# Second layer's routing of a two-layer transformer kernel: the first eight token tiles' deviations, normalisation, transposes and router products placed in the tail of the second attention

## The chip, the cores and the metric

The kernel runs on one core of one Trainium2 chip. The metric is the device time of one execution in microseconds. Three runs of the kernel before gave a median of 1085.19 us (1085.11 to 1086.78). One more execution was recorded by the profiler: it took 1081.04 us, of which 1079.3 us lie between its first and its last instruction (the span). All rows below are of that execution, and their times count from the span's start.

Engines: PE is TensorE (matmuls and transposes; PEld its weight loads), DVE VectorE, ACT ScalarE, POOL GpSimd, SP SyncE (it issues the plain transfers).

## The reference, cut to what matters

2048 tokens of 256 channels (8 sequences of 256) pass through two layers, each an attention over a small context and a mixture of experts with a shared expert:

```python
x = x + tanh(g_xattn[0]) * xattn0(layernorm(x), ctx)       # linear attention
x = x + tanh(g_ffn[0])   * ffn0(layernorm(x))              # 8 experts, top 2
x = x + tanh(g_xattn[1]) * xattn1(layernorm(x), ctx)       # 16 heads, quantised softmax attention
x = x + tanh(g_ffn[1])   * ffn1(layernorm(x))              # 16 experts, top 4

def layernorm(x): return (x - mean(x)) / sqrt(var(x) + 1e-5)

def ffn1(x):
    logits = x @ router_w.T                     # 16 logits a token
    vals, idx = top_k(softmax(logits), 4)       # weights of the chosen experts
    shared = silu(x @ sgate.T) * (x @ sup.T) @ sdown.T
    return sum over the 4 chosen experts(w * expert(x)) + sigmoid(x @ se_gate.T) * shared
```

The change concerns the seam between `xattn1` and `ffn1`: the last `layernorm`, and `logits`.

## The kernel before

**Tiles.** The tokens are 16 tiles of 128 (`NT` = 16); `x_sb` holds them all, 128 partitions by 16 tiles by 256 channels. Each engine has its own program, written out by hand in Python; the order of the calls is the order on the engine, and the engines meet only at semaphores. No scheduler moves anything.

**The second attention** (`attn1_pe`, `attn1_act`, `attn1_dve`, `attn1_pool`) is a software pipeline of 136 steps `s`. A step stands for two heads of one tile (`PAIRS` = 8, so eight steps a tile, 128 steps `NQ` of heads, eight of run-out). In a step PE computes the logits of two heads (L1178) and transposes the probabilities of an earlier step (L1188) and multiplies them with the values (L1200), DVE finds the maxima (L1303) and copies transposed probabilities (L1308), ACT takes the exponentials (L1262), and POOL rounds them to integers (L1606), twice a step. Beside this, once in 16 steps, a pair of tiles `G` gets its queries ready (POOL L1554 to L1579, PE L1082 to L1099), and a pair of tiles `o` is finished: `normalised` divides by the sums (L1313, L1315), PE transposes (L1210), ACT and DVE split into high and low halves (`output_high` L1273, `output_low` L1322), PE projects (`project`, L256 and L263), DVE adds the result to x (`update`, L1328) and takes its mean and variance (`stats`, L240 and L243). `output_step(s, j, tail)` says in which step a pair has its turn; the last pair, `o` = 7, is taken in the run-out at `s = NQ + tail`. POOL also splits the second layer's weights into halves, a third of an item in each step in which it has no queries to do (L1407 to L1412), until they run out.

**The seam.** After the last `update` and `stats`, DVE adds the epsilon (`stats_end`, L247), POOL raises to the power -1/2 (`inverse_deviation`, L1679), and `route_dve`, `route_act`, `route_pe` do the routing. First DVE makes `nmr`, minus mean by deviation, for all 16 tiles (L419). Then, for each of eight pairs of tiles `j`: ACT normalises the even tile (L403) and DVE the odd one (L422) into `xnf`; PE transposes both (four fp32 transposes, L359) into PSUM bank `j % 2`; ACT copies the high halves into `xnT` (L407), DVE subtracts for the low halves (L430); PE multiplies with the router's weights (`mm3`, 12 matmuls of 17 columns, L256), and DVE copies the logits to `lg` (L434). SP stores each pair of normalised tiles to the token table in HBM. Before the routing PE, ACT and DVE meet at a barrier: `meet(…, 3)` is a drain and a wait for the other two.

**After it** the shared expert's gate and up products (`shared_gate_up`, L256 on `sgu`) start once all eight pairs' logits are copied (`r_lgc`), beside DVE's choice of experts (`choose_dve` and what follows, L446 to L566), after which the gathers for the experts start on POOL (L631).

Of the kernel before, what the change touches and what calls it, by code (L numbers as in the profile page):

```python
# [10 lines left out]
ALU = mybir.AluOpType  # L11
# [4 lines left out]
C = D // P  # L16
HEADS, HD = 16, 16
MAGIC = 1.5 * 2.0 ** 23
SW = 256.0
# [13 lines left out]
def gated_flamingo(nc, a, out):  # L33
# [30 lines left out]
    with ExitStack() as ctx:  # L64
# [184 lines left out]
        EARLY = LATE = 4  # L249
        STATS_STEPS = (4, 8, 14)  # L250
# [99 lines left out]
        def route_pe(pe, l):  # L350
            n = E[l] + 1
            for j in range(NT // 2 + 1):
                if j < NT // 2:
                    at_least(pe, r_xn[l], 0, j + 1)
                    at_least(pe, r_xd[l], 0, j + 1)
                    at_least(pe, r_xl[l], 0, j - 1)
                    for c in range(C):
                        for i in range(2):
                            last = nc.tensor.transpose(PS[:, j % 2, c * TB + i * P:c * TB + (i + 1) * P],  # L359
                                                       xnf[:, 2 * j + i, c * P:(c + 1) * P], idf[:, :])  # L360
                    last.then_inc(r_xT[l].sem, 1)
                if j >= 1:
# [34 lines left out]
        def route_act(act, l):  # L397
            act.wait_ge(rstd_ready, 2 + 3 * l)
            at_least(act, r_nm[l], 0, 1)
            for j in range(NT // 2 + 1):  # L400
                if j < NT // 2:
# [3 lines left out]
                if j >= 1:  # L405
# [10 lines left out]
        def route_dve(dve, l):  # L416
            n = E[l]
            dve.wait_ge(rstd_ready, 2 + 3 * l)
            nc.vector.scalar_tensor_tensor(nmr[:, :], mv[:, :, 0], -1.0, rstd[:, :], ALU.mult, ALU.mult)\  # L419
                .then_inc(r_nm[l].sem, 1)  # L420
            def normalise(t):
                nc.vector.tensor_scalar(xnf[:, t, :], x_sb[:, t, :], mv[:, t, 0:1], rstd[:, t:t + 1],  # L422
                                        ALU.subtract, ALU.mult).then_inc(r_xd[l].sem, 1)
            normalise(1)
            for j in range(NT // 2 + 1):
                if j + 1 < NT // 2:
                    normalise(2 * j + 3)
                if j < NT // 2:
                    at_least(dve, r_xh[l], 0, j + 1)
                    nc.vector.tensor_tensor(xnT[:, 1, :, j * TB:(j + 1) * TB], PS[:, j % 2, :].rearrange("p (c n) -> p c n", c=C),  # L430
                                            xnT[:, 0, :, j * TB:(j + 1) * TB], ALU.subtract).then_inc(r_xl[l].sem, 1)
                if j >= 1:
                    at_least(dve, r_lg[l], 0, j)
                    nc.vector.tensor_scalar(lg[:, 2 * j - 2:2 * j, 0:n + 1],  # L434
                                            PS[:, 2 + (j - 1) % 2, 0:2 * (n + 1)].rearrange("p (i e) -> p i e", i=2),
                                            1 / SW, None, ALU.mult).then_inc(r_lgc[l].sem, 1)
# [733 lines left out]
        def attn1_pe(pe):  # L1170
# [82 lines left out]
            meet(pe, 3)  # L1253

        def attn1_act(act):
# [39 lines left out]
            meet(act, 3)  # L1295

        def attn1_dve(dve, combine):
# [32 lines left out]
            for s in range(STEPS):  # L1330
# [27 lines left out]
                o = output_step(s, 18, 7)  # L1358
                if o is not None:
                    stats(2 * o, 2 * o + 1)  # L1360
            stats_end(0, NT)
            meet(dve, 3)
# [239 lines left out]
        def attn1_pool(pl, inverse_deviation):  # L1602
# [7 lines left out]
            for s in range(NQ):  # L1610
                integers(s)
                if s == 3:
                    inverse_deviation(3, EARLY, NT)
                if all(query_step(s, j) is None for j in (0, 8, 9, 10, 11)) and parts < 3 * len(items):
                    split_part(pl, parts // 3, parts % 3)
                    parts += 1
# [14 lines left out]
        def _(pl):  # L1631
# [56 lines left out]
            inverse_deviation(4)  # L1688
# [6 lines left out]
        def _(act):  # L1695
# [90 lines left out]
            route_act(act, 1)  # L1786
# [3 lines left out]
        def _(dve):  # L1790
# [124 lines left out]
            route_dve(dve, 1)  # L1915
# [3 lines left out]
        def _(pe):  # L1919
# [105 lines left out]
            route_pe(pe, 1)  # L2025
# [49 lines left out]
```

## Time and profile before

| what | value |
|---|---|
| median of 3 runs | 1085.19 us |
| profiled execution | 1081.04 us |
| its span | 1079.3 us |
| PE busy | 855.4 us, 79% of the span |
| DVE busy | 751.1 us, 70% |
| POOL busy | 644.7 us, 60% |
| ACT busy | 460.2 us, 43% |
| chain that ended last, by engine | PE 40%, POOL 18%, DVE 13%, issue 10% |
| of it at L359 (routing transposes) | PE 1% |
| of it at L1606 (POOL's integers, `sb_wk` and `sb_wkh`) | 3% |

Busy time is an average over stages that differ: the share of an engine in the span tells nothing of who holds up the seam. The second attention lies from about 370 us to 716 us, the routing from 722 us to 736 us, the choice of experts to 785 us. The chain of work that ended last is the view that tells, at each moment, whose work the end waited for; the timeline of an engine gives for each group of instructions its start, its length, and in brackets how long the engine idled before and what released it.

### The profile page before, as it was taken

What the parts mean: (1) busy time and instruction counts of PE and PEld (TensorE: products, weight loads), DVE (VectorE), ACT (ScalarE), POOL (GpSimd) and SP (SyncE); (2) the same over time, 40 slices, a digit from 0 to 9 for tenths busy, and PEclk for the clock granted to TensorE, in tenths of its full rate; (3) what the DMA queues carried; (4) which work ended last, traced back from release to release, by engine and by line L of the source; (5) the groups of instructions that cost most, each with busy time, mean ns of one, the idle gap of its engine ahead of it and who ended that gap; (6) DMA issues with size and microseconds to landing.
All of it is one profiled execution on the core that took longest, in us unless ns stands there. A gap on an engine that the chain in (4) does not pass through costs nothing.

```text
span 1079.3 us, 21036 instructions
## 1 busy us (share of the span) xinstructions
PE 855.4 (79%) x6928; PEld 572.4 (53%) x6929; DVE 751.1 (70%) x1527; ACT 460.2 (43%) x993; POOL 644.7 (60%) x851
## 2 busy tenths in 40 slices
PE   4489668699989877787777787859769999997764
PEld 2267545477655444445445455535557777763432
DVE  5779667467567777797787787947956767754445
ACT  3455244233222357666657666825123333321201
POOL 4586781667275878888888887610054444415563
PEclk9689759799999856687786786857679999997988
DMA  7021142244321100000110000011024444423341
GB/s 249 25 77 34 56 125 63 76 142 150 112 87 50 47 15 14 15 21 22 28 41 25 16 4 1 2 39 40 6 83 136 126 136 124 139 81 97 98 117 59
DMA packets 55445, 75.04 MB, mean 70 GB/s; under 512 B 11069, under 2 KB 46657, under 8 KB 55361
## 3 DMA queue, kind: packets, MB, share of 16 engines
q1 hardware_dynamic: 44992, 44.82, 13.0%
q0 software_dynamic: 10368, 29.14, 10.0%
q8 instruction: 48, 0.79, 0.3%
q14 instruction: 37, 0.30, 0.1%
HBM read 51.45 MB, written 22.49 MB: 69 GB/s over the span
## 4 chain that ended last, share of the span: by engine, by line
PE 40%; POOL 18%; DVE 13%; issue 10%; ACT 5%; POOLq 5%; DVEq 4%; DMA 2%; another core or an unknown queue 1%; SPq 0%; ACTq 0%
PE PS L256 24%; PE PS L679 3%; POOL sb_xnf L656 3%; POOL sb_xnf L631 3%; DVE sb_slotv L1303 3%; POOL sb_wk L1606 2%; PE PS L703 2%; PE PS L732 2%; PE PS L1188 2%; PE PS L1178 2%; ACT sb_wk L1262 2%; POOL sb_wkh L1606 1%; POOL sb_region L1412 1%; PE PS L359 1%; DMA sb_x_sb<-x 1%
## 5 line engine op out<-in xcount | busy, mean ns | idle before, releaser
L631 POOL DMA_INDIRECT sb_xnf<-token_table,sb_ids x120 | 115.8, 965 | 180.1 <-DVE sb_ids L565 87.9
L256 PE MATMUL PS<-sb_region,sb_wkh 88*128 (+1 forms) x1440 | 210.7, 297 | 5.4 <-issue 2.8
L1303 DVE TENSOR_REDUCE sb_slotv<-PS 128x1 f32<-128x512 f32 x256 | 164.0, 683 | 42.6 <-PE PS L1178 42.6
L256 PEld LDWEIGHTS PS<-sb_region,sb_wkh 88*128 88x128 f16 (+1 forms) x1440 | 136.9, 99 | 57.9 <-issue 12.8
L656 POOL DMA_INDIRECT sb_xnf<-slot_table,sb_place x96 | 96.5, 1005 | 90.6 <-DMA slot_table<-sb_wa 39.0
L256 PE MATMUL PS<-sb_xnT,sb_sgu 128*128 128x512 f16 x528 | 132.0, 402 | 2.1 <-issue 1.1
L679 PE MATMUL PS<-sb_sdn,sb_wkh 128*128 128x256 f16 (+1 forms) x576 | 79.5, 293 | 46.5 <-DVE sb_wkh L846 32.6
L1262 ACT ACTIVATE sb_wk<-PS,sb_slotv 128x512 f32<-128x512 f32 x128 | 86.9, 686 | 36.8 <-DVE sb_slotv L1303 33.6
L761 ACT ACTIVATE sb_wk<-PS 128x512 f32<-128x512 f32 (+1 forms) x48 | 28.6, 595 | 166.9 <-PE PS L256 139.4
L679 PEld LDWEIGHTS PS<-sb_sdn,sb_wkh 128*128 128x128 f16 (+1 forms) x576 | 57.1, 103 | 70.9 <-DVE sb_wkh L846 41.6
L1606 POOL TENSOR_SCALAR sb_wk<-sb_wk 128x512 f32<-128x512 f32 x128 | 79.5, 621 | 20.5 <-ACT sb_wk L1262 11.7
L256 PEld LDWEIGHTS PS<-sb_xnT,sb_sgu 128*128 128x128 f16 x528 | 53.3, 103 | 68.2 <-issue 19.6
L1308 DVE TENSOR_SCALAR sb_wkh<-PS 128x1024 f16<-128x1024 f16 x112 | 76.9, 687 | 10.5 <-PE PS L1200 9.8
L780 ACT ACTIVATE sb_wkh<-PS 128x512 f16<-128x512 f32 x60 | 35.8, 596 | 106.9 <-PE PS L703 97.1
L875 DVE SCALAR_TENSOR_TENSOR sb_wk<-PS,sb_sm,sb_wk 128x176 f32<-128x176 f32 x120 | 42.6, 397 | 51.7 <-ACT sb_wk L789 45.6
L839 DVE SCALAR_TENSOR_TENSOR sb_wk<-PS,sb_wk 128x512 f32<-128x512 f32 (+1 forms) x48 | 33.2, 692 | 64.5 <-ACT sb_wk L761 52.9
L1188 PE MATMUL PS<-sb_idh,sb_wk 128*128 128x128 f16 x512 | 58.8, 270 | 12.2 <-POOL sb_wk L1606 6.7
L789 ACT ACTIVATE sb_wk<-PS 128x352 f32<-128x352 f32 x60 | 27.8, 463 | 88.8 <-PE PS L256 75.4
L859 DVE TENSOR_TENSOR sb_wkh<-PS,sb_wkh 128x512 f16<-128x512 f32 x60 | 41.4, 690 | 33.1 <-ACT sb_wkh L780 32.0
L1188 PEld LDWEIGHTS PS<-sb_idh,sb_wk 128*128 128x128 f16 x512 | 39.6, 119 | 40.6 <-issue 32.8
L1262 ACT ACTIVATE sb_wkh<-PS,sb_slotv 128x512 f32<-128x512 f32 x64 | 43.4, 683 | 29.9 <-DVE sb_slotv L1303 29.2
L1412 POOL TENSOR_TENSOR sb_region<-sb_stg,sb_region 128x704 f16<-128x704 f32 (+1 forms) x32 | 43.0, 1344 | 20.9 <-issue 19.9
(281 smaller groups left out, 1816.1 us busy)
## 6 DMA issues: line engine op xcount, KB each, us to landing
slot_table<-sb_wa SPq DMA_DIRECT2D x60, 256.0 KB
sb_stg<-gu SPq DMA_DIRECT2D x24, 352.0 KB, 3.0
sb_stg<-dn SPq DMA_DIRECT2D x24, 176.0 KB
token_table<-sb_xnf SPq DMA_DIRECT2D x16, 256.0 KB, 3.6
sb_stg<-sgu SPq DMA_DIRECT2D x8, 352.0 KB, 6.6
sb_x_sb<-x SPq DMA_DIRECT2D x1, 2048.0 KB, 12.1
out<-sb_x_sb SPq DMA_DIRECT2D x16, 128.0 KB
sb_xnf<-token_table,sb_ids POOLq DMA_INDIRECT x120
```

Of the source, the lines that this page charges most:

```text
L256: last = nc.tensor.matmul(out_, lhs(i, c), rhs(j, c), start=(c == 0 and n == 0 and not begun), stop=(c == C - 1 and n == 2 and not more))
L631: nc.gpsimd.indirect_dma_start(xg[l][:, 2 * (g % XR) + n, :], None, xw[l][:, :], bass.IndirectOffsetOnAxis(ap=ids[:, 2 * g + n:2 * g + n + ...
L656: nc.gpsimd.indirect_dma_start(yr[l][r][:, k, :], None, ys[l][:, :], bass.IndirectOffsetOnAxis(ap=place[:, k, t:t + 1], axis=0))\
L679: last = nc.tensor.matmul(PS[:, 4 + i // 2, i % 2 * D:(i % 2 + 1) * D], wkh[0:r, HR * h + v, i * P:(i + 1) * P], sdn[0:r, j, k, :], start= ...
L859: nc.vector.tensor_tensor(wkh[:, 2 * (s % 2) + 1, :], PS[:, 4 + s % 2, :], wkh[:, 2 * (s % 2), :], ALU.subtract).then_inc(e_xl[l].sem, 1)
L875: last = nc.vector.scalar_tensor_tensor(wk1[:, 2 + u, n * EI:(n + 1) * EI], PS[:, 2 * u + n, EI:EG], wv[u][:, n:n + 1], wk1[:, u, n * EI:( ...
L1188: last = nc.tensor.transpose(bank[:, (h * KT + k) * P:(h * KT + k + 1) * P], h_p[s % NE][:, h, k * P:(k + 1) * P], idh[:, :])
L1262: nc.scalar.activation(h_e[s % NE][:, h, :], PS[:, 2 * u + h, :], ACT.Exp, bias=h_nb[u][:, h:h + 1], accum_out=o_sum[v][:, head:head + 1]) ...
L1303: nc.vector.tensor_reduce(h_nb[u][:, h:h + 1], PS[:, 2 * u + h, :], AX, ALU.max, negate=True).then_inc(h_max, 1)
L1308: nc.vector.tensor_scalar(h_T[s % 2], PS[:, 4 + s % 2, :].bitcast(F16), -RB, None, ALU.add).then_inc(h_pc_dve, 1)
L1412: nc.gpsimd.tensor_tensor(lo, w, hi, ALU.subtract).then_inc(stg_split[n % 4], 1)
L1606: nc.gpsimd.tensor_scalar(h_e[s % NE][:, h], h_e[s % NE][:, h], 255.0, MAGIC + RB_BITS, ALU.mult, ALU.add).then_inc(h_int, 1)
```

## The change

The routing is cut into two halves of four pairs. `route_pe`, `route_act` and `route_dve` take a first and an end pair. The first half (tiles 0 to 7) stands at the end of the attention functions, in the place of the barrier `meet(…, 3)`; the second half (tiles 8 to 15) stands where the whole stood. For the first half:

- DVE closes the variances of tiles 0 to 7 (`stats_end(0, 8)`) in step 83, after `stats` of pair 3;
- POOL raises them to the power -1/2 in step 90, between the integers and the query work of that step; the second call, for tiles 8 to 15, is where the call for all tiles was;
- in step 133 (`NQ + 5`), between `output_low(7)` and `update(7)`, DVE makes `nmr` of tiles 0 to 7 and normalises the four odd tiles; the low halves and logits of the four pairs come after the last `stats_end`;
- ACT's and PE's first half follow `output_high(7)` and `project(7)`.

`stats` of a pair `o` below 7 moves from step 18 + 16(o+1) to the next step, so that it stands behind `normalised` rather than before it.

```diff
@@ -247,6 +247,7 @@
...
+        ROUTE_EARLY = 8
@@ -347,10 +348,10 @@
...
-        def route_pe(pe, l):
+        def route_pe(pe, l, first=0, end=NT // 2):
...
-            for j in range(NT // 2 + 1):
-                if j < NT // 2:
+            for j in range(first, end + 1):
+                if j < end:
@@ -359,7 +360,7 @@
...
-                if j >= 1:
+                if j > first:
@@ -394,15 +395,15 @@
...
-        def route_act(act, l):
-            act.wait_ge(rstd_ready, 2 + 3 * l)
-            at_least(act, r_nm[l], 0, 1)
-            for j in range(NT // 2 + 1):
-                if j < NT // 2:
+        def route_act(act, l, first=0, end=NT // 2):
+            act.wait_ge(rstd_ready, 2 + 3 * l + (first > 0))
+            at_least(act, r_nm[l], 0, 1 + (first > 0))
+            for j in range(first, end + 1):
+                if j < end:
...
-                if j >= 1:
+                if j > first:
@@ -413,27 +414,34 @@
...
-        def route_dve(dve, l):
+        def deviations_route(dve, l, first, end):
+            dve.wait_ge(rstd_ready, 2 + 3 * l + (first > 0))
+            nc.vector.scalar_tensor_tensor(nmr[:, first:end], mv[:, first:end, 0], -1.0, rstd[:, first:end], ALU.mult, ALU.mult)\
+                .then_inc(r_nm[l].sem, 1)
+
+        def normalise_dve(l, t):
+            nc.vector.tensor_scalar(xnf[:, t, :], x_sb[:, t, :], mv[:, t, 0:1], rstd[:, t:t + 1],
+                                    ALU.subtract, ALU.mult).then_inc(r_xd[l].sem, 1)
+
+        def low_logits_dve(dve, l, j, first, end):
...
+            if j < end:
+                at_least(dve, r_xh[l], 0, j + 1)
+                nc.vector.tensor_tensor(xnT[:, 1, :, j * TB:(j + 1) * TB], PS[:, j % 2, :].rearrange("p (c n) -> p c n", c=C),
+                                        xnT[:, 0, :, j * TB:(j + 1) * TB], ALU.subtract).then_inc(r_xl[l].sem, 1)
+            if j > first:
+                at_least(dve, r_lg[l], 0, j)
+                nc.vector.tensor_scalar(lg[:, 2 * j - 2:2 * j, 0:n + 1],
+                                        PS[:, 2 + (j - 1) % 2, 0:2 * (n + 1)].rearrange("p (i e) -> p i e", i=2),
+                                        1 / SW, None, ALU.mult).then_inc(r_lgc[l].sem, 1)
+
+        def route_dve(dve, l, first=0, end=NT // 2):
+            deviations_route(dve, l, 2 * first, 2 * end)
+            normalise_dve(l, 2 * first + 1)
+            for j in range(first, end + 1):
+                if j + 1 < end:
+                    normalise_dve(l, 2 * j + 3)
+                low_logits_dve(dve, l, j, first, end)
@@ -1250,7 +1258,7 @@
...
-            meet(pe, 3)
+            route_pe(pe, 1, 0, ROUTE_EARLY // 2)
@@ -1292,7 +1300,7 @@
...
-            meet(act, 3)
+            route_act(act, 1, 0, ROUTE_EARLY // 2)
@@ -1355,11 +1363,18 @@
...
-                o = output_step(s, 18, 7)
+                o = output_step(s, 19 + 0, 7)
...
-            stats_end(0, NT)
-            meet(dve, 3)
+                if o == ROUTE_EARLY // 2 - 1:
+                    stats_end(0, ROUTE_EARLY)
+                if s == NQ + 5:
+                    deviations_route(dve, 1, 0, ROUTE_EARLY)
+                    for t in range(1, ROUTE_EARLY, 2):
+                        normalise_dve(1, t)
+            stats_end(ROUTE_EARLY, NT)
+            for j in range(ROUTE_EARLY // 2 + 1):
+                low_logits_dve(dve, 1, j, 0, ROUTE_EARLY // 2)
@@ -1611,6 +1626,8 @@
...
+                if s == (ROUTE_EARLY // 2 + 1) * GSTEPS + 10:
+                    inverse_deviation(4, 0, ROUTE_EARLY)
@@ -1685,7 +1702,7 @@
...
-            inverse_deviation(4)
+            inverse_deviation(5, ROUTE_EARLY, NT)
@@ -1783,7 +1800,7 @@
...
-            route_act(act, 1)
+            route_act(act, 1, ROUTE_EARLY // 2)
@@ -1912,7 +1929,7 @@
...
-            route_dve(dve, 1)
+            route_dve(dve, 1, ROUTE_EARLY // 2)
@@ -2022,7 +2039,7 @@
...
-            route_pe(pe, 1)
+            route_pe(pe, 1, ROUTE_EARLY // 2)
```

On DVE, from `update` of pair 6 to the first odd tiles (names: `sb_slotv` are the sums' reciprocals, `sb_xnT` in L1315 and L1323 the attention's output, `sb_ve` variance plus epsilon). Before:

```order
L1328 SCALAR_TENSOR_TENSOR sb_x_sb<-PS,sb_tgw,sb_x_sb 128x512 [waits o_y]
L240 BN_STATS sb_bst<-sb_x_sb 128x6 x2
L243 BN_AGGR sb_mv<-sb_bst 128x2 x2
L1313 RECIPROCAL sb_slotv<-sb_slotv 128x16 [waits o_T,h_pv]
L1315 TENSOR_TENSOR sb_xnT<-PS,sb_slotv 128x256
L1322 SCALAR_TENSOR_TENSOR sb_xnT<-PS,sb_xnT 128x512 [waits o_y,o_hi]
L1328 SCALAR_TENSOR_TENSOR sb_x_sb<-PS,sb_tgw,sb_x_sb 128x512 [waits o_y]
L240 BN_STATS sb_bst<-sb_x_sb 128x6 x2
L243 BN_AGGR sb_mv<-sb_bst 128x2 x2
L247 TENSOR_SCALAR sb_ve<-sb_mv 128x16
L419 SCALAR_TENSOR_TENSOR sb_nmr<-sb_mv,sb_rstd 128x16 [waits rstd_ready,phase]
```

and with the change:

```order
L1336 SCALAR_TENSOR_TENSOR sb_x_sb<-PS,sb_tgw,sb_x_sb 128x512 [waits o_y]
L1321 RECIPROCAL sb_slotv<-sb_slotv 128x16 [waits o_T,h_pv]
L1323 TENSOR_TENSOR sb_xnT<-PS,sb_slotv 128x256
L240 BN_STATS sb_bst<-sb_x_sb 128x6 x2
L243 BN_AGGR sb_mv<-sb_bst 128x2 x2
L1330 SCALAR_TENSOR_TENSOR sb_xnT<-PS,sb_xnT 128x512 [waits o_y,o_hi]
L419 SCALAR_TENSOR_TENSOR sb_nmr<-sb_mv,sb_rstd 128x8 [waits rstd_ready]
L423 TENSOR_SCALAR sb_xnf<-sb_x_sb,sb_mv,sb_rstd 128x256 x4
L1336 SCALAR_TENSOR_TENSOR sb_x_sb<-PS,sb_tgw,sb_x_sb 128x512 [waits o_y]
L240 BN_STATS sb_bst<-sb_x_sb 128x6 x2
L243 BN_AGGR sb_mv<-sb_bst 128x2 x2
L247 TENSOR_SCALAR sb_ve<-sb_mv 128x8
```

The two rows of `normalised` (L1313, L1315; now L1321, L1323) stand ahead of the statistics of pair 6, and `nmr` with four odd tiles stands ahead of the last `update`; the barrier (`phase`) is gone.

On DVE, the routing of the pairs after that. Before, each pair's odd tile is normalised between the low halves:

```order
L422 TENSOR_SCALAR sb_xnf<-sb_x_sb,sb_mv,sb_rstd 128x256 x2
L430 TENSOR_TENSOR sb_xnT<-PS,sb_xnT 128x2x256 [waits r_xh]
L422 TENSOR_SCALAR sb_xnf<-sb_x_sb,sb_mv,sb_rstd 128x256
L430 TENSOR_TENSOR sb_xnT<-PS,sb_xnT 128x2x256 [waits r_xh]
L434 TENSOR_SCALAR sb_lg<-PS 128x34 [waits r_lg]
L422 TENSOR_SCALAR sb_xnf<-sb_x_sb,sb_mv,sb_rstd 128x256
```

With the change the low halves and logits of four pairs follow one another, and then the second half begins with its own `nmr`, which can't start before the last logits of the first half are copied:

```order
L430 TENSOR_TENSOR sb_xnT<-PS,sb_xnT 128x2x256 [waits r_xh] x2
L434 TENSOR_SCALAR sb_lg<-PS 128x34 [waits r_lg]
L430 TENSOR_TENSOR sb_xnT<-PS,sb_xnT 128x2x256 [waits r_xh]
L434 TENSOR_SCALAR sb_lg<-PS 128x34 [waits r_lg]
L430 TENSOR_TENSOR sb_xnT<-PS,sb_xnT 128x2x256 [waits r_xh]
L434 TENSOR_SCALAR sb_lg<-PS 128x34 [waits r_lg] x2
L419 SCALAR_TENSOR_TENSOR sb_nmr<-sb_mv,sb_rstd 128x8 [waits rstd_ready]
L423 TENSOR_SCALAR sb_xnf<-sb_x_sb,sb_mv,sb_rstd 128x256 x2
```

On POOL, step 90 of the attention (L1606, now L1621, are the integers; L1564 to L1568, now L1579 to L1583, the rounding of queries). Before:

```order
L1606 TENSOR_SCALAR sb_xnf<-sb_xnf 128x512 [waits h_exp] x2
L1564 TENSOR_SCALAR sb_xnT<-sb_xnT 128x256 [waits q_frac]
L1566 TENSOR_SCALAR sb_xnT<-sb_xnT 128x256
L1568 TENSOR_TENSOR sb_xnT<-sb_xnT,sb_slotv 128x256
L1606 TENSOR_SCALAR sb_wkh<-sb_wkh 128x512 [waits h_exp] x2
L1577 TENSOR_SCALAR sb_xnT<-sb_xnT 128x16x16 [waits q_T]
```

and with the change, one instruction more:

```order
L1621 TENSOR_SCALAR sb_xnf<-sb_xnf 128x512 [waits h_exp] x2
L1696 TENSOR_TENSOR sb_rstd<-sb_ve,sb_mhalf 128x8 [waits stats_ready]
L1579 TENSOR_SCALAR sb_xnT<-sb_xnT 128x256 [waits q_frac]
L1581 TENSOR_SCALAR sb_xnT<-sb_xnT 128x256
L1583 TENSOR_TENSOR sb_xnT<-sb_xnT,sb_slotv 128x256
L1621 TENSOR_SCALAR sb_wkh<-sb_wkh 128x512 [waits h_exp] x2
L1592 TENSOR_SCALAR sb_xnT<-sb_xnT 128x16x16 [waits q_T]
```

## Rows read from the trace of the kernel before

**Rows 1.** Stretches: us; busy and count by engine; granted clock, DMA share, GB/s.

```profile
420.00:670.00 250.00, 193.85 (x2032) 124.60 (x2031) 201.54 (x358) 165.94 (x416) 213.55 (x341) 0.75 0.07 20
670.00:702.00 32.00, 26.75 (x327) 17.27 (x325) 31.69 (x58) 25.66 (x69) 20.34 (x33) 0.89 0.01 2
```

**Rows 2.** Timeline of POOL, steps 90, 91: start, length, idle before, releaser.

```profile
617.71 1.31 POOL L1606 TENSOR_SCALAR sb_xnf<-sb_xnf 128x512 f32<-128x512 f32 x2
...
620.89 1.31 POOL L1606 TENSOR_SCALAR sb_wkh<-sb_wkh 128x512 f32<-128x512 f32 x2
```

**Rows 3.** Chain of waits, end of step 91: start, length, instruction.

```profile
623.30 0.68 POOL sb_xnT L1579
624.02 1.04 PE PS L1099 x8
```

**Rows 4.** Timeline of DVE, end of the attention and the routing.

```profile
707.13 0.75 DVE L1328 SCALAR_TENSOR_TENSOR sb_x_sb<-PS,sb_tgw,sb_x_sb 128x512 f32<-128x512 f32 x1 [1.06 <-PE PS L263]
707.98 0.75 DVE L240 BATCH_NORM_STATS2 sb_bst<-sb_x_sb 128x6 f32<-128x256 f32 x2
...
708.97 0.22 DVE L1313 RECIPROCAL sb_slotv<-sb_slotv 128x16 f32<-128x16 f32 x1
709.26 0.42 DVE L1315 TENSOR_TENSOR sb_xnT<-PS,sb_slotv 128x256 f32<-128x256 f32 x1
...
716.23 0.75 DVE L1328 SCALAR_TENSOR_TENSOR sb_x_sb<-PS,sb_tgw,sb_x_sb 128x512 f32<-128x512 f32 x1 [4.02 <-PE PS L263]
...
718.58 0.17 DVE L247 TENSOR_SCALAR sb_ve<-sb_mv 128x16 f32<-128x16 f32 x1 [0.43 <-issue]
721.86 0.18 DVE L419 SCALAR_TENSOR_TENSOR sb_nmr<-sb_mv,sb_rstd 128x16 f32<-128x16 f32 x1 [3.10 <-POOL sb_rstd L1679]
...
724.60 0.69 DVE L430 TENSOR_TENSOR sb_xnT<-PS,sb_xnT 128x512 f16<-128x512 f32 x1 [1.92 <-ACT sb_xnT L407]
...
735.92 0.19 DVE L434 TENSOR_SCALAR sb_lg<-PS 128x34 f32<-128x34 f32 x1 [0.48 <-PE PS L256]
```

**Rows 5.** Timeline of PE, the last projections and the routing.

```profile
712.27 1.46 PE L256 MATMUL PS<-sb_wqp,sb_xnT 128*128 128x256 f16 x6 [1.41 <-DVE sb_xnT L1322]
...
722.85 1.94 PE L359 MATMUL PS<-sb_idf,sb_xnf 128*128 128x128 f32 x8 [6.65 <-ACT sb_xnf L403]
...
725.71 1.09 PE L359 MATMUL PS<-sb_idf,sb_xnf 128*128 128x128 f32 x4
...
731.65 1.09 PE L359 MATMUL PS<-sb_idf,sb_xnf 128*128 128x128 f32 x4
```

**Rows 6.** POOL's power by shape: count, busy, mean ns, idle before.

```profile
L1679 POOL TENSOR_TENSOR sb_rstd<-sb_ve,sb_mhalf 128x4 f32<-128x4 f32 x1 | 1.1, 1127 | 0.0
...
L1679 POOL TENSOR_TENSOR sb_rstd<-sb_ve,sb_mhalf 128x12 f32<-128x12 f32 x1 | 2.3, 2306 | 0.1
```

**Rows 7.** Timeline of PE, logits of step 115.

```profile
678.26 0.39 PE L1178 MATMUL PS<-sb_wkv,sb_xnT 64*128 64x512 f16 x1 [0.28 <-ACT sb_xnf L1262]
```

**Rows 8.** Chain of waits, first gate and up product of layer 1.

```profile
736.17 5.31 PE PS L256 x12
```

**Rows 9.** Stretches in which the granted clock rose, layer 1 and layer 0.

```profile
740.00:742.00 2.00, 2.00 (x6) 0.73 (x5) 0.00 (x0) 0.49 (x1) 0.00 (x0) 0.52 0.00 0
...
158.00:162.00 4.00, 4.00 (x11) 1.43 (x10) 3.33 (x6) 0.00 (x0) 3.64 (x5) 0.54 1.11 340
```

**Rows 10.** Timeline of PE, first gate and up product of layer 0.

```profile
157.36 3.17 PE L256 MATMUL PS<-sb_xnT,sb_sgu 128*128 128x512 f16 x7 [0.27 <-DVE sb_lg L434]
```

**Rows 11.** Timeline of PE, a later gate and up product of layer 1.

```profile
753.01 2.75 PE L256 MATMUL PS<-sb_xnT,sb_sgu 128*128 128x512 f16 x12
```

More of the change, by code:

```diff
@@ L414, in softmax_act @@
             nc.scalar.activation(sm[:, 1, :], lg[:, :, E[l]], ACT.Exp, scale=-1.0).then_inc(r_exp[l].sem, 1)
-        def route_dve(dve, l):
-            n = E[l]
[L418 to L436, printed above, removed]
```

## The prediction

> **What bounds the kernel now.** I read the chain of waits first, then the timeline of each engine at the two places where instructions are put in.
>
> At the seam the chain hops between engines. The last projections of the attention begin at 712.27 [rows 5], `update(7)` waits 4.02 us for them and starts at 716.23, `stats_end` ends at 718.75, POOL's power keeps DVE idle for 3.10 us, and `nmr` starts at 721.86 [rows 4]. PE has then idled 6.65 us and starts its first routing transposes at 722.85 [rows 5]. The last logits are copied at 735.92 + 0.19 = 736.11 [rows 4], and the first gate and up product starts at 736.17 [rows 8]. The eight pairs run in two PSUM banks: pair 2's transposes start at 725.71 and pair 6's at 731.65 [rows 5], so four pairs take 5.94 us, 1.485 us each. That is latency from engine to engine, not one engine's work.
>
> In the attention itself POOL sets the pace until its weight splits run out: from 420 to 670 us it is busy 213.55 of 250 us, more than DVE's 201.54 or PE's 193.85; from 670 to 702 us it has only 20.34 us of work in 32, and DVE is busy for 31.69 [rows 1]. Step 90, where the change puts the power of eight columns, starts at 617.71, step 91 at 620.89, and neither shows idle time before it [rows 2]. The chain of waits passes through POOL's last query instruction of step 91 at 623.30 and PE's transposes at 624.02 that waited for it [rows 3].
>
> **The seam, term by term.** The barrier costs nothing now: it is over while POOL computes the power. Nor is its removal worth anything, except that work may stand before it.
>
> First, `normalised` goes ahead of the statistics of pair 6. Those hold DVE from 707.98 to 708.97, where the reciprocal starts; the divided tile starts at 709.26 and everything up to `update(7)` hangs on it [rows 4]. Without them the reciprocal starts at 707.98, so the tail moves up by 0.99 us: projections from 711.3, `update(7)` at 715.24 instead of 716.23, `stats_end` over at 717.76. The moved statistics lie beside PE's transposes and ACT's copy. `nmr` and the four odd tiles (some 0.4 us each, before `update(7)`) lie beside the projections, which take 3.9 us; ACT's first two tiles too.
>
> Second, the first half. PE's transposes of pairs 0 and 1 follow the projections directly: 715.2 to 717.2, by the 1.94 us that these eight take now [rows 5]. DVE comes to the low half of pair 0 after `stats_end`, at about 717.8. From there to the last logits it now takes 736.11 - 724.60 = 11.51 us for eight pairs [rows 4]; four pairs less are 5.94 us less, so 5.57 us, until 723.35. POOL's power for tiles 8 to 15 is done by 719.6 and hidden.
>
> Third, the second half starts afresh, since its `nmr` is queued on DVE behind the last logits of the first. From `nmr` to the transposes takes 722.85 - 721.86 = 0.99 us as now, and from the transposes to the last logits 13.26 - 5.94 = 7.32 us [rows 4, 5]. It ends at 723.35 + 0.99 + 7.32 = 731.7, against 736.11: 4.4 us gained. Had the halves been joined without restart, it would be some 2 us more; this restart is what the cut gives back.
>
> **The attention, term by term.** The power of eight columns doesn't occur in the trace. Its nearest rows are four columns at 1127 ns and twelve at 2306 ns [rows 6]; halfway is 1.72 us, and with a gap of 0.07 us between POOL instructions 1.8 us. On an engine without idle time at that place, and with the chain through its next query instructions, it delays everything behind it in full, since PE's transposes at 624.02 wait for it and DVE and ACT wait for PE. I charge 1.8 us. The bounds are 0 (hidden in a POOL idle later on) and 2.4 us (the twelve-column row and a gap). It also splits the later power, whose saving is not counted, being hidden.
>
> The statistics of pairs 0 to 5 move by a step too. In steps 35 to 99 POOL is the pace, and I charge nothing: DVE's total is the same, and they fill a step in which DVE has no probabilities to copy. In step 115 DVE is the pace [rows 1]: it comes to the maxima 0.99 us earlier and finds the second head's logits ready only at 678.26 + 0.39 = 678.65 [rows 7]. I charge 0.2 us; bounds -0.3 (smoother) to +0.5.
>
> **The clock.** PE's first gate and up product is on the chain, 5.31 us for 12 matmuls [rows 8]; a later one takes 2.75 [rows 11]. The granted clock averages 0.52 of full speed over 740 to 742 [rows 9], so it rose from 1.2 to 2.4 GHz at about 741.9, 5.7 us after the product began. In layer 0 the same product began at 157.36 [rows 10] and the average over 158 to 162 is 0.54, a rise at 161.7, 4.3 us after [rows 9]. Were it 1.4 us earlier here, work done in that time would go twice as fast, 0.7 us saved. I take 0.3 us of gain, bounds -0.7 to +0.7.
>
> **The sum.** -4.4 + 1.8 + 0.2 - 0.3 = -2.7 us. Against the profiled execution's own 1081.04 us that is 1078.3. The median of the three timed runs is 1085.19, 4.15 us above it, so I forecast 1082.5 us. What a measurement of this kernel can tell from no change is about 0.2%, 2.2 us: faster is below 1083.0, slower above 1087.4. The forecast lies half a microsecond from that edge.
>
> **Rivals.**
>
> *The clock comes early.* Projections and the transposes of pairs 0 and 1 now make 3.9 + 1.94 = 5.9 us of unbroken PE work, as long as the stretch of gate and up after which the clock rose. PE's 6.65 us of idleness between them is gone. At 2.4 GHz the transposes (0.97 us a pair) and router products (about 0.5 us) of a pair of pairs would be 0.7 us shorter on the chain; six remaining pairs give 2.1, and the first gate and up product 5.31 - 2.75 = 2.6. Then the time is 1082.5 - 4.7 = 1077.8. Against it: the routing of today, PE busy at most times from 722.85 on, did not raise it. The Trainium skill, "TensorE: Matmul & The Clock Gate", Part 1, says that the throttled clock is the default and sustained activity releases it. By that rule the unbroken stretch speaks for this rival; the trace agrees in so far as the rise came within gate and up.
>
> *The power is hidden.* If POOL's idle time after step 103 took up the delay, 1.8 us come back: 1080.7. For it: POOL has 11.66 us of idleness from 670 to 702 [rows 1]. Against it: PE waited for POOL's query work before that, and DVE, the pace from 670 on, waits for PE.
>
> *The gain is eaten without a loss.* The power costs 2.4, step 115 0.5, the clock rises late (+0.7): -4.4 + 3.6 = -0.8, 1084.4.
>
> *Slower: the statistics delay the next maxima.* In each of six steps 16k + 3 DVE now has the division and 0.99 us of statistics before the maxima of the next step, on which ACT's exponentials and POOL's integers hang. If none of it is covered by what was gained a step earlier, 6 x 0.99 = 5.9 us, and the time is 1082.5 - 0.2 + 5.9 = 1088.2. It decides from 0.45 us a step (the gain of 2.7 is gone then). For it: DVE is busy 81% of the time even where POOL is the pace. Against it: the statistics stood before a maximum already, one step earlier, and the step behind has no more work than it had.
>
> **How the numbers follow.** Forecast 0.60, with its own range 1080.9 to 1084.2; clock early 0.12; power hidden 0.08; gain eaten 0.12; slower 0.08. Of the forecast's 0.60 I put 0.36 below 1083.0; with 0.11 of the early clock and 0.07 of the hidden power, faster is 0.54. Slower is 0.06, the rest, 0.40, is within 0.2%. The range 1079.0 to 1086.5 leaves out the far ends of the early clock and of the slower case.
>
> **What would show it.** Right: a power of about 1.7 us on POOL in step 90, and steps from 91 on later by as much, to the last maxima; then PE's first fp32 routing transposes directly behind the last projections; a pause of PE of about 1.3 us before the first router product and of about 1.5 us between the halves; first gate and up product 4.4 us earlier relative to the attention's last maxima. Wrong: POOL idle behind step 90 that shrinks by the power's length, maxima of steps 36, 52 and so on that start later than their logits, a clock of 2.4 GHz within the routing, or a second half that starts without waiting for the first.

## The result, and the profile after

The changed kernel took 1075.70 us (median of 20 runs, 1071.44 to 1084.90), the kernel before 1081.68 us beside it (20 runs, 1075.83 to 1086.78). The ratio is 0.9959, 95% interval 0.9940 to 0.9978, or -4.4 us (-6.5 to -2.4). A second measurement, described below, gave 0.9997 (0.9963 to 1.0031). Weighted by their intervals the two make 0.9968 (0.9951 to 0.9985), -3.4 us. The profiled execution took 1071.44 us (span 1069.7), by chance the shortest of its runs; 5.5 of the 9.6 us by which it is ahead of the profiled execution before lie ahead of the second attention (POOL's first integers at 367.70, before at 373.16), where nothing was changed.

DVE's timeline of the changed kernel, from `update` of pair 6 to the end of the routing (start, length, group, idle before and releaser):

```profile
706.87 0.75 DVE L1336 SCALAR_TENSOR_TENSOR sb_x_sb<-PS,sb_tgw,sb_x_sb 128x512 f32<-128x512 f32 x1 [0.23 <-PE PS L264]
707.54 0.24 DVE L1321 RECIPROCAL sb_slotv<-sb_slotv 128x16 f32<-128x16 f32 x1
...
714.37 0.75 DVE L1336 SCALAR_TENSOR_TENSOR sb_x_sb<-PS,sb_tgw,sb_x_sb 128x512 f32<-128x512 f32 x1 [2.65 <-PE PS L264]
...
716.44 1.28 DVE L430 TENSOR_TENSOR sb_xnT<-PS,sb_xnT 128x512 f16<-128x512 f32 x2
...
720.86 0.19 DVE L434 TENSOR_SCALAR sb_lg<-PS 128x34 f32<-128x34 f32 x1 [0.48 <-PE PS L257]
720.97 0.16 DVE L419 SCALAR_TENSOR_TENSOR sb_nmr<-sb_mv,sb_rstd 128x8 f32<-128x8 f32 x1
...
729.06 0.19 DVE L434 TENSOR_SCALAR sb_lg<-PS 128x34 f32<-128x34 f32 x1 [0.49 <-PE PS L257]
```

The reciprocal now starts 0.67 us after `update(6)`; before it was 708.97 - 707.13 = 1.84 [rows 4]. From `update(7)` to the last logits it is 14.88 us against 19.88. The 3.10 us of idleness before `nmr` [rows 4] are gone: the second half's `nmr` has no idle time in front of it, but it stands, as forecast, behind the first half's last logits.

PE's timeline there:

```profile
708.33 0.66 PE L1218 MATMUL PS<-sb_idf,sb_xnT 128*128 128x128 f32 x4 [1.01 <-DVE sb_xnT L1323]
...
713.73 0.60 PE L264 MATMUL PS<-sb_brow,sb_ones_h 1*128 1x256 f16 x2
714.26 1.90 PE L360 MATMUL PS<-sb_idf,sb_xnf 128*128 128x128 f32 x8
717.18 0.46 PE L257 MATMUL PS<-sb_rw,sb_xnT 128*128 128x17 f16 x12 [1.03 <-DVE sb_xnT L430]
717.50 0.64 PE L360 MATMUL PS<-sb_idf,sb_xnf 128*128 128x128 f32 x4
...
721.88 1.97 PE L360 MATMUL PS<-sb_idf,sb_xnf 128*128 128x128 f32 x8 [1.05 <-ACT sb_xnf L404]
...
724.77 1.09 PE L360 MATMUL PS<-sb_idf,sb_xnf 128*128 128x128 f32 x4
```

The first transposes follow the projections without a gap, where PE idled for 6.65 us [rows 5]. Four transposes take 0.64 us at 717.50 and 1.09 at 724.77: for a while TensorE ran at 2.4 GHz. So it did in the first row, the attention's own transposes of pair 7, which take 0.66 us here and 1.12 in the kernel before. The granted clock (the last figure but two), in stretches of 1 us:

```profile
716.00:717.00 1.00, 0.16 (x2) 0.00 (x0) 0.89 (x4) 1.00 (x4) 0.38 (x1) 1.00 0.00 0
...
719.00:720.00 1.00, 0.45 (x12) 0.40 (x12) 1.00 (x3) 0.55 (x1) 0.00 (x0) 0.69 0.19 55
```

It is at full speed from 716.0, behind PE's unbroken stretch that began at 710.41, until some 719.4. On POOL, step 90 now holds the power:

```profile
616.04 1.32 POOL L1621 TENSOR_SCALAR sb_xnf<-sb_xnf 128x512 f32<-128x512 f32 x2
617.44 1.65 POOL L1696 TENSOR_TENSOR sb_rstd<-sb_ve,sb_mhalf 128x8 f32<-128x8 f32 x1
...
620.98 1.32 POOL L1621 TENSOR_SCALAR sb_wkh<-sb_wkh 128x512 f32<-128x512 f32 x2
```

The step takes 4.94 us against 3.18 [rows 2]. The routing's last copy releases the first gate and up product, on the chain of waits:

```profile
729.06 0.20 DVE sb_lg L434
...
729.31 4.59 PE PS L257 x12
```

It takes 4.59 us, 0.72 less than before [rows 8]. That is no gain of the change: in the three other profiles of the kernel before (below) the same product takes 4.2 to 5.0 us, in those of the changed kernels 4.0 to 5.3, as the granted clock rises sooner or later within it.

### The profile page after: what moved, and what is told of

Its sections match the earlier page's. It is cut to its first block, busy times and chain, and to the rows that moved or that the text cites. A ratio compares the mean times of both kernels' runs of the same rounds, so it can differ in the third digit from the quotient of the medians.

```text
span 1069.7 us, 21037 instructions
## 1 busy us (share of the span) xinstructions
PE 849.5 (79%) x6928; PEld 572.6 (54%) x6929; DVE 755.6 (71%) x1529; ACT 462.2 (43%) x993; POOL 645.5 (60%) x852
## 4 chain that ended last, share of the span: by engine, by line
PE 35%; POOL 18%; DVE 15%; issue 11%; ACT 5%; POOLq 5%; DVEq 4%; another core or an unknown queue 4%; DMA 3%; SPq 0%; ACTq 0%
PE PS L257 21%; POOL sb_xnf L639 3%; DVE sb_slotv L1311 3%; POOL sb_xnf L664 2%; POOL sb_wk L1621 2%; PE PS L687 2%; PE PS L740 2%; PE PS L711 2%; POOL sb_region L1427 2%; PE PS L1196 2%; PE PS L1186 2%; ACT sb_wk L1270 1%; POOL sb_wkh L1621 1%; DMA sb_x_sb<-x 1%
## 5 line engine op out<-in xcount | busy, mean ns | idle before, releaser
L257 PE MATMUL PS<-sb_xnT,sb_sgu 128*128 128x512 f16 x528 | 127.8, 395 | 1.1 <-DVE sb_lg L434 0.6
L1621 POOL TENSOR_SCALAR sb_wk<-sb_wk 128x512 f32<-128x512 f32 x128 | 79.8, 623 | 24.1 <-ACT sb_wk L1270 15.4
```

The source lines that it names most:

```text
L257: last = nc.tensor.matmul(out_, lhs(i, c), rhs(j, c), start=(c == 0 and n == 0 and not begun), stop=(c == C - 1 and n == 2 and not more))
L1621: nc.gpsimd.tensor_scalar(h_e[s % NE][:, h], h_e[s % NE][:, h], 255.0, MAGIC + RB_BITS, ALU.mult, ALU.add).then_inc(h_int, 1)
```

## The experiments

After the first measurement (row "changed") came three groups of runs, each on its own chip beside runs of the kernel before: 1079.46 us in the first (changed again, power late, statistics only, gap), 1081.66 in the second (before again, four early tiles, halves joined, statistics back), 1057.26 in the third (the last two rows and two single executions of the kernel before). Ratios compare within a group. Each kernel also left one profile. *Tail* is from `update(6)` to the reciprocal, *routing* from `update(7)` to the first gate and up product, *attention* from POOL's first integers to those of step 127.

| kernel | ratio to before (95%) | tail | routing | step 90 | attention |
|---|---|---|---|---|---|
| before, page shown ahead | | 1.84 | 19.94 | 3.18 | 329.1 |
| before again, second group | 1.0001 (0.9970-1.0033) | 1.83 | 19.95 | 3.19 | 332.6 |
| before, two executions, third group | | 1.84, 1.83 | 19.94 | 3.20, 3.19 | 335.1, 333.6 |
| changed | 0.9959 (0.9940-0.9978) | 0.67 | 14.94 | 4.94 | 335.3 |
| changed again | 0.9997 (0.9963-1.0031) | 0.67 | 15.89 | 4.93 | 337.8 |
| power late | 0.9949 (0.9914-0.9984) | 0.67 | 14.92 | 3.19 | 336.4 |
| statistics only | 1.0015 (0.9979-1.0050) | 0.67 | 19.95 | 3.21 | 334.4 |
| gap on PE | 0.9988 (0.9951-1.0026) | 0.67 | 16.41 | 4.92 | 337.6 |
| four early tiles | 0.9977 (0.9938-1.0016) | 0.67 | 15.95 | 3.19 | 337.1 |
| statistics back, power late | 0.9958 (0.9927-0.9990) | 1.83 | 15.90 | 3.20 | 334.8 |
| halves joined, power late | 0.9960 (0.9923-0.9997) | 0.67 | 13.15 | 3.19 | 336.9 |
| joined, again | 0.9942 (0.9914-0.9971) | 0.67 | 13.14 | 3.19 | 337.1 |
| joined, only pair 6's statistics | 0.9925 (0.9895-0.9956) | 0.67 | 13.63 | 3.20 | 332.2 |

The medians have intervals of 3 to 4 us each way; the columns from the profiles, tail, routing and step 90, repeat within 0.05 us as long as the clock is the same. So the steps of the argument are judged by the profiles.

**The changed kernel again.**

> The changed kernel once more, for a second profile. Theory A (the gain is latency taken off the seam, and a single execution differs by when the clock is granted): step 90 on POOL again takes 1.7 to 1.8 us more than step 106; from the start of POOL's last integers to the first gate and up product 26.5 to 29.5 us against 33.9 before; and the time before the second attention differs from the first profile by some us with nothing changed there. Theory B (the change also shortens something outside the seam, as the 5.4 us that this profile was ahead at the attention's start would suggest): the start of the attention is again some 5 us earlier than before's. Time 3 to 6 us under before.

1079.26 us, a ratio of 0.9997. Its routing shows no rise of the clock, and so is 0.95 us longer than in the first profile:

```profile
714.00:721.00 7.00, 4.58 (x21) 2.19 (x22) 3.94 (x13) 1.69 (x3) 0.00 (x0) 0.65 0.22 76
721.00:737.00 16.00, 11.29 (x130) 9.21 (x130) 9.68 (x28) 8.88 (x15) 1.65 (x1) 0.50 0.29 99
```

The granted clock stays at 0.50 throughout the routing. The early clock is thus not a property of the changed program: of eight profiles with the unbroken stretch on PE it came in four. In these four the clock had last fallen 5.2 to 5.4 us before `update(7)`; in the other four 4.5 to 4.9 or 6.2 to 6.4 us before it. The expectation's theory B falls: the attention starts at 370.31 us here, in the four profiles of the kernel before at 365.5 to 373.2.

**Power late.** Power of tiles 0 to 7 behind POOL's last integers:

```diff
-                if s == (ROUTE_EARLY // 2 + 1) * GSTEPS + 10:
-                    inverse_deviation(4, 0, ROUTE_EARLY)
...
+            inverse_deviation(4, 0, ROUTE_EARLY)
             inverse_deviation(5, ROUTE_EARLY, NT)
```

> POOL's power of tiles 0 to 7 stands behind the last integers, where POOL is idle, rather than in step 90. If the power in step 90 delays all behind it (the prediction's term of 1.8 us): step 90 takes 3.2 us as before and the kernel is 1.8 us faster than the changed one, some 0.55 to 0.6% under before. If POOL's idle time later on hides it: the same time as the changed kernel.

1074.45 us. Step 90 falls back to 3.19 us and the seam stays as it was (14.92), so in the attention the power cost 1.75 us and in the tail it costs nothing: POOL idles there. The kernel is 4.8 us under the changed kernel of its group, where 1.8 were expected; the intervals of the two overlap, so the times neither show the 1.8 us nor contradict them.

**Statistics only.** The kernel before with one number changed:

```diff
-                o = output_step(s, 18, 7)
+                o = output_step(s, 19, 7)
```

> The kernel before with one edit: the statistics of pairs 0 to 6 one step later. If the prediction's term holds: the division of tile 15 starts 0.3 us after the update of pair 6 ends rather than 1.4, the seam is 1.0 us shorter, steps 115 and 116 together are within 0.3 us of before, total 0.7 to 1.0 us faster (0.1%). If the statistics delay the next maxima (the slower rival): steps 35, 51, 67, 83, 99 show up to 0.99 us more each on POOL and the kernel is 2 to 5 us slower. If the order also spares steps outside the tail, it is over 1.5 us faster.

1080.94 us: no difference that this can tell. The maxima that the slower rival named are not late: POOL's steps 35, 51, 67, 83 and 99, and the step behind each, are as long as in the kernel before, within 0.02 us in all fourteen profiles. Step 54 is longer, 3.24 us, where it takes 2.89 to 2.92 at the same clock with the statistics in their old place (more on it below). The tail is 1.17 us shorter and the routing as before, so the remaining 4.0 to 5.0 us of the seam belong to the early half alone.

**Gap on PE.** PE's first half waits for the last `update`:

```diff
+            at_least(pe, o_x, 0, GROUPS)
             route_pe(pe, 1, 0, ROUTE_EARLY // 2)
```

> The changed kernel, but PE waits for the last update before the first routing transposes, so that projections and transposes no longer make one unbroken stretch (a pause of 0.8 us between). If the unbroken stretch is what raised the clock within the routing: the granted clock stays at half (1.2 GHz) until the gate and up product, the first half takes 5.6 us from the first low half to the last logits rather than 4.5, and the seam is 1.2 to 1.7 us longer than in the changed kernel. If the rise was chance of the moment: it comes here as often, and the seam differs only by the 0.4 us that the first low half starts later.

1079.49 us. PE waits 0.85 us, the clock doesn't rise, the routing takes 16.41 us, 0.52 more than the changed kernel's at the same clock. (Its profile is of its longest run, 1088.86 us.) The order of transposes directly behind projections is worth half a microsecond. Whether the gap prevented a rise can't be said: without it the rise came only half of the time, and the clock had last fallen 4.8 us before `update(7)` here, as in the changed kernel's second profile (4.9), in which there was no gap and no rise either.

**The kernel before itself.**

> The kernel before, submitted as a kernel of its own: what the comparison says of no change, and a second profile of it. If the attention's length is a matter of when the clock is granted: from POOL's first to its last integers 332 to 338 us as in the five kernels with the statistics moved, not 329.07 as in its first profile. If the moved statistics cost the attention some 5 us (the prediction's slower rival): again 329 to 330. Ratio 1.000 within its interval.

1083.90 us beside 1081.66: the ratio is 1, as it must be, but the attention of one and the same program took 332.6 us here and 329.1 in the first profile. That is inside the range expected of the clock alone and above the 329 to 330 expected of a cost of 5 us.

**Four early tiles.** `ROUTE_EARLY = 4` for 8, the power in step 58.

> The changed kernel with four early tiles for eight: two pairs in the first half, six in the second, the early power (four columns) in step 58. By the prediction's sum the number of early pairs doesn't matter as long as they cover the later power: update of pair 7 to first gate and up product 15.9 us without and 14.9 with the early clock, as with eight tiles, and the power delays the attention by 1.2 rather than 1.8 us. If the gain were the work placed early, half of it would be lost: 17.5 to 18 us.

1080.03 us. The power of four columns adds 1.10 us to step 58, and the routing takes 15.95 us, as long as with eight tiles (15.89 at the same clock). What the cut gains is not the amount of work placed early, but that there is some: it covers `stats_end` and the power of the other tiles, during which PE and DVE idled before.

**Halves joined.** Power late, and the eight pairs in one pipeline. PE and ACT have one call for all pairs, and DVE makes the second `nmr` and odd tiles between the low halves:

```diff
-            for j in range(ROUTE_EARLY // 2 + 1):
-                low_logits_dve(dve, 1, j, 0, ROUTE_EARLY // 2)
+            for j in range(NT // 2 + 1):
+                if j == 2:
+                    dve.wait_ge(rstd_ready, 6)
+                    nc.vector.scalar_tensor_tensor(nmr[:, ROUTE_EARLY:NT], mv[:, ROUTE_EARLY:NT, 0], -1.0,
+                                                   rstd[:, ROUTE_EARLY:NT], ALU.mult, ALU.mult).then_inc(r_nm[1].sem, 1)
+                if ROUTE_EARLY <= 2 * j + 3 < NT:
+                    normalise_dve(1, 2 * j + 3)
+                low_logits_dve(dve, 1, j, 0, NT // 2)
```

> The power late as in e1, and the two halves joined: the second half's deviations stand behind the first logits, so that eight pairs run in one pipeline without a restart. If the restart costs what the prediction says: the last logits 11.5 us after the first low half, update of pair 7 to gate and up 13.4 to 13.9 us against 15.9, total 2 us under e1 and 5.5 to 6 us (0.5%) under before. If the later power or the order on DVE holds it up: 15 us or more.

1075.93 us. The routing takes 13.15 us, 1.77 less than with the restart and the same early clock. The time shows none of it: 0.9960 beside the 0.9949 of power late, where 2 us less were expected, and the intervals are 3 to 4 us wide each way. DVE's timeline in its repetition:

```profile
717.99 0.17 DVE L1382 SCALAR_TENSOR_TENSOR sb_nmr<-sb_mv,sb_rstd 128x8 f32<-128x8 f32 x1 [0.41 <-POOL sb_rstd L1703]
```

The second `nmr` waits 0.41 us for POOL, all that is left of the 3.10 us [rows 4].

**Statistics back, power late.** `output_step(s, 18, 7)` again in the changed kernel.

> The power late as in e1, and the statistics of pairs 0 to 6 back in their old step. If the tail's term holds: the update of pair 6 to the division of tile 15 takes 1.84 us again rather than 0.67, all else as e1: 1.2 us slower than e1. If the moved statistics cost the attention 5 us: from first to last integers 329 to 331 us rather than e1's 336.4, and the kernel is 3 to 4 us faster than e1.

1077.79 us, 0.9958. The tail is 1.83 us again and the routing 15.90: the two parts of the seam's gain are independent. The attention takes 334.8 us, neither the 329 to 331 that a cost of 5 us asked for nor the 336.4 of power late.

**Only pair 6's statistics moved**, in the joined kernel:

```diff
-                o = output_step(s, 19 + 0, 7)
+                o = output_step(s, 18, 7)
+                if o == GROUPS - 2:
+                    o = None
+                if output_step(s, 19, 7) == GROUPS - 2:
+                    o = GROUPS - 2
```

> The halves are joined in one pipeline of eight pairs, the power of tiles 0 to 7 stands behind POOL's last integers, and only pair 6's statistics stand a step later; those of pairs 0 to 5 stand in the place they have in the kernel before. Theory 1 (the later statistics of pairs 0 to 5 cost nothing, the attention's length differs by the clock's phase alone): the attention from POOL's first integers to its last takes 329 to 337 us as in the other kernels without the early power, the last update comes 6.8 us after the reciprocal and the first gate and up product about 13.2 us after the last update, and the time is that of the joined kernel, 0.995 to 0.997 of before. Theory 2 (the later statistics delay the maxima of steps 16k+4): the attention is 2 us or more shorter than in the joined kernel (336.9 us) and the ratio is below 0.994.

1050.36 us, 0.9925, the best ratio of all. With all statistics moved:

> The joined kernel once more: the halves joined, the power of tiles 0 to 7 behind the last integers, all statistics a step later. Last update to gate and up 13 to 14 us, ratio to before 0.994 to 0.998. Against the kernel with only pair 6's statistics moved: no difference by theory 1 (clock's phase), 2 us or more slower by theory 2 (later statistics cost).

1051.40 us, 0.9942. The ratio 0.9925 and an attention 4.9 us shorter are what theory 2 asked for, but the intervals overlap, and 2.6 of the 4.9 us lie in steps 102 and 103 (7.64 and 5.06 us), whose clock also differs between two runs of one program (below). Of the rest, 0.9 us lie in step 71 (4.10 and 3.21) and 0.4 in step 8, ahead of any moved statistics, and 0.4 in steps 110 and 111, which are short in this profile alone, for a reason that wasn't found. Neither theory holds as it stands: the later statistics do cost something, but not by the maxima. What they do shows in DVE's timeline, here with the statistics in their old place:

```profile
510.24 0.75 DVE L240 BATCH_NORM_STATS2 sb_bst<-sb_x_sb 128x6 f32<-128x256 f32 x2
...
512.40 0.24 DVE L1324 RECIPROCAL sb_slotv<-sb_slotv 128x16 f32<-128x16 f32 x1
...
514.86 0.69 DVE L1128 TENSOR_TENSOR sb_xnT<-PS,sb_xnT 128x512 f16<-128x512 f32 x1
```

and with all of them a step later:

```profile
502.62 1.29 DVE L1314 TENSOR_REDUCE sb_slotv<-PS 128x1 f32<-128x512 f32 x2 [0.48 <-PE PS L1189]
503.82 0.24 DVE L1324 RECIPROCAL sb_slotv<-sb_slotv 128x16 f32<-128x16 f32 x1
...
504.65 0.75 DVE L240 BATCH_NORM_STATS2 sb_bst<-sb_x_sb 128x6 f32<-128x256 f32 x2
...
507.41 0.68 DVE L1128 TENSOR_TENSOR sb_xnT<-PS,sb_xnT 128x512 f16<-128x512 f32 x1
```

From the reciprocal to L1128, DVE's part of the next queries, it is 3.59 us instead of 2.46, and against POOL's integers of step 52 (516.52 and 508.50) L1128 is 0.57 us later: in the old place the rest of their 0.99 us filled a wait for PE, the 0.48 us that now stand in the first row. At the end of the queries, steps 54 and 55 take 7.36 us here and 7.01 there, both with the clock at 1.2 GHz. All fourteen profiles together:

| step | statistics moved (8 profiles) | in the old place (6) |
|---|---|---|
| 54, clock low | 3.21 to 3.28 (7) | 2.89 to 2.92 (4) |
| 54, clock full | 2.72 (1) | 2.72 (2) |
| 86 | 2.55 to 2.59 (5), 2.23 or 2.24 (3) | 2.23 or 2.24 (6) |
| 101 to 103, clock low | 9.26 to 9.65 (6), 10.19 (1) | 9.01 to 9.29 (3) |
| 101 to 103, clock full | 6.99 (1) | 6.92 or 6.93 (3) |

For steps 101 to 103 the clock's moments matter too; in the two profiles in which it falls and rises at the same moments within 0.1 us, they take 9.43 (gap on PE) and 9.29 (the kernel before, the first of the two executions below). So the later statistics cost up to about 0.9 us in sum where the clock is low (0.35, 0.3 and 0.15 to 0.35), and next to nothing in the changed kernel's first profile, where it was full at the first and the last. The profiles show this, the medians don't. Two more executions of the kernel before,

> The kernel before once more, for the length of its attention. Theory 1 (the clock's phase sets it): anything from 329 to 336 us, with the steps 22, 23, 54, 55, 86, 87, 102, 103 at either of their lengths (2.8 or 4.1 us for step 103). Theory 2 (the later statistics make it long): 329 to 333 us, and step 55 at 2.7 us as in both traces of before so far.

> As the look at the kernel before that runs ahead of it: 329 to 336 us by theory 1, 329 to 333 us by theory 2.

took 1056.74 and 1063.46 us, with attentions of 335.1 and 333.6 us: longer than the 333 that theory 2 allowed. Step 55, 2.7 us in the first two traces of this program, takes 4.09 in both; step 103 takes 4.09 in one and 2.83 in the other. Steps 102 and 103 of the first, then of the second (the last figure but two is the granted clock):

```profile
642.71:650.14 7.43, 5.10 (x60) 2.78 (x58) 5.61 (x11) 2.68 (x9) 3.54 (x6) 0.90 0.00 0
```

```profile
647.76:652.82 5.06, 2.89 (x47) 1.87 (x44) 4.84 (x10) 2.31 (x7) 3.54 (x6) 1.00 0.01 3
```

2.37 us apart. In the first the granted clock was 0.50 from about 637.4 to 644.3, in the second it stayed at 1.00 throughout. All fourteen profiles follow this: steps 54 and 55 take 5.4 us where the clock was full from 2 us ahead of them, and 6.8 to 7.4 where it was low (6.1 once, when it rose just before).

## Why the prediction was right or wrong

**The level was wrong.** The forecast was a change of -2.7 us on a base of 1085.19; measured were 1075.70, outside the range. The change is within both intervals, -4.4 (-6.5 to -2.4) and the pooled -3.4. What failed is the step "the median of the three timed runs is 1085.19, 4.15 us above it", which set the profiled execution's 1081.04 aside: beside the changed kernel the same program took 1081.68 (20 runs, of which those three are the first), and 1079.46, 1081.66 and 1057.26 in the later groups. Single runs of it spread over 11 to 19 us within a group, so three that agree within 1.7 us don't fix a median. Of the miss of 6.8 us, 3.5 are this base, 1.7 the change by the ratio (-4.4 for -2.7), and the last 1.6 the difference between a difference of medians (-6.0) and the ratio. The range held the unknowns of the change and nothing for the base.

**Tail, forecast -0.99, measured -1.17** in every kernel with pair 6's statistics moved. The old distance from `update(6)` to the reciprocal was 1.84; the sum took off the statistics alone and kept 0.85 for `update`, after which the reciprocal now starts at 0.67. The sum left the way from the reciprocal to `update(7)` as it was, 7.26 us. It takes 6.83 in eight of the nine profiles in which pair 6's statistics stand behind the division, since the four transposes on it (L1218; L1210 in the kernel before) run at 2.4 GHz there, 0.66 us for 1.12; in the ninth it takes 7.20 and in the five others 7.17 to 7.27. These 0.4 us are a gain that the forecast doesn't have.

**Routing, forecast -3.4, measured -4.05 at 1.2 GHz** (19.94 to 15.89 in the repetition). The first half's last logits come 7.64 us after `update(7)` there and 8.11 in the sum: `stats_end` followed the aggregate after 0.43 us of idleness [rows 4], now after 0.07, and the low half starts 2.08 us after `update(7)`, not 2.56. The second half takes 8.25 us to the gate and up product, forecast 8.3. The mechanism and its order were right, the restart too: put at "some 2 us", it costs 2.26 at 1.2 GHz (15.89 against 13.63) and 1.77 with the early clock.

**Power in step 90, forecast 1.8, measured 1.75,** and paid in full: the attention did not take it up in POOL's idle time (steps 104 to 125 take 48.09 us, before 48.05), and moving it to the tail gave step 90 back its 3.19 us. The rival of the hidden power falls.

**Statistics of pairs 0 to 5, forecast 0 before step 100 and 0.2 in step 115.** Steps 114 to 116 take 6.58 us in both. But steps 54, 86 and 101 to 103 pay up to about 0.9 us together at the low clock. L1128, which comes 0.57 us later, is the likely way; no run moved it alone. The step that failed here is "I charge nothing" for steps 35 to 99: the reason given, that DVE's total is the same, leaves out what else stands behind the statistics on DVE. The slower rival had a cost of this kind at 5.9 us, and by the maxima, which didn't move.

**Clock, forecast -0.3.** The early rise came in half of the profiles. It took 0.95 us off the routing (15.89 against 14.94). The rival's 4.7 us were too many: the clock had fallen again at 719.4, before the second half, and the gate and up product began at 1.2 GHz. The 0.72 us that this product was shorter are within what it varies by in the kernel before (5.31, 4.7, 4.2 and 5.0 us), so the forecast's -0.3 can't be judged. The rule of the Trainium skill, "TensorE: Matmul & The Clock Gate", Part 1, that sustained activity releases the throttled clock, agrees with the rise at 716.0; the runs add that the same stretch of PE work was followed by a rise in one execution and not in another.

**The sum of the measured terms**, at the low clock, is -1.17 - 4.05 + 1.75 + 0.9 = -2.6 us; with the 0.4 us of pair 7's transposes it is -3.0, and with the early rise in the routing -3.9. Forecast -2.7: that it is so near is luck, since too small a gain in the seam and too small a cost in the attention cancelled. The interval of the pooled -3.4 us (-5.2 to -1.7) holds all three.

**What stays open.** In the eight profiles with all statistics moved the attention averages 335.8 us, its early power (1.75 or 1.10) taken off; in the six with them in place 332.9. That is 2.9 us, at most 0.9 of it accounted for above. The rest lies in how often the query steps met the low clock (steps 54 and 55 in seven of eight against four of six, 102 and 103 in seven of eight against three of six). Whether the moved statistics bring the low clock about or this is chance, these profiles can't tell.

The best kernel is the joined one with the power late and only pair 6's statistics moved, 0.9925 (0.9895 to 0.9956) of before; that it beats the joined one with all of them moved is not shown by the times.

## What to carry to other kernels

Where a seam idles all engines for a short serial chain (a statistic, a power, a normalisation), a few tiles of later work put in front are enough to cover it; ask then what restarts the pipeline behind them, and join the parts. A small instruction on an engine that sets the pace costs its full length: put it where that engine already idles. One that an engine has time for can still cost, by what stands behind it in that engine's order: look at what waits for the next instructions too. And before a forecast of a time, ask how well its base is known: a change of 3 us is lost among single runs that spread over 16.

## What the runs showed of the hardware

The attention of one program takes 329.1 to 335.1 us in four profiles. The 6.0 us between the first and the longest lie in nine steps (22, 23, 54, 55, 71, 87, 102, 103, 126); all others agree within 0.1 us together. Two of the nine, 102 and 103, take 5.06 us with the granted clock at 1.00 and 7.43 where it was at 0.50 ahead of them. The power on POOL takes 1651 ns for 128x8, between 1127 for four columns and 2306 for twelve [rows 6]. On the third chip the kernel before was 22 to 24 us faster, and 18 to 20 us of this lie behind the choice of experts: from there to the end it takes 274.2 and 275.8 us in its two profiles, against 294.7 and 294.3 in those of the other chips. Its attention took no less. The cause wasn't looked for.
